# Attention output projection from 16-bit high and low parts; row maxima as bias of one exponential per head on ScalarE

## The chip, the cores and the metric

The kernel runs on one core of a Trainium2 chip. The metric is the device time of one execution in microseconds (us). The engines are named as the profile names them: PE (TensorE), PEld (its weight loads), DVE (VectorE), ACT (ScalarE), POOL (GpSimd) and SP (SyncE, which issues most of the DMAs).

## The reference

A graph network of four layers over 2048 nodes with 512 features, each with layer norm and ReLU ahead of it and a residual sum behind it. The change touches the first layer alone, an attention over 32 graphs of 64 nodes with 8 heads of 64 features. `eb` is a bias per edge, added to the scores at the edge's place.

```
h = jnp.maximum(_layernorm(x, axis=-1), 0.0)
q = (h @ Wq + bq).reshape(32, 64, 8, 64)      # k and v alike
attn = jnp.einsum('bnhd,bmhd->bnmh', q, k) * scale
attn = attn.at[b_idx, loc_src, loc_dst].add(eb)
attn = jax.nn.softmax(attn, axis=2)
out = jnp.einsum('bnmh,bmhd->bnhd', attn, v).reshape(2048, 512)
x = x + out @ Wo + bo
```

Three graph convolutions follow, each a product with a 512 x 512 weight and a sum over edges by dense 2048 x 2048 matrices that the kernel builds itself.

## The kernel before

The program has three stretches. First it reads the edges, builds count, weight and bias matrices and projects q, k and v (to about 424 us of the span). Then comes the attention. Then come the layers, which are long runs of 16-bit matmuls.

The attention works on 16 tiles of 128 nodes (two graphs each). Its order is written out by hand as a pipeline: `attention_periods` runs t from -4 to 16, and in each period every engine does a fixed list of steps for different tiles, with semaphores between them. In period t

- PE turns the probabilities of tile t+1 (`turn`, L1628), projects the output of tile t with Wo (`output`, L1658), mixes the values of tile t+1 (`mix`, L1646) and makes the scores of tile t+4 (`scores`, L1617);
- ACT copies the turned probabilities of tile t+1 from PSUM (`copy_turned`, L1556), takes the exponential of tile t+3 (`exponentials`, L1550), and copies the mixed values of tile t+1 with the bias bv added (`copy_mixed`, L1565), which makes `att_t`, the stationary operand of the output projection;
- DVE makes the probabilities of tile t+2 (sum, reciprocal, product, a copy of one head: L1708 to L1717), adds the edge bias to the scores of tile t+3, reduces their maxima per row and head and subtracts them (L1692, L1697, L1700), and adds the projected output of tile t-1 to x with its layer norm statistics (`add_out`, L1723 to L1728);
- POOL adds the row bo to x (L1541).

An engine takes its list in order: a step that waits holds back all that stands behind it. The probabilities have four buffers (`m.prob[:, t % 4]`), `att_t` has one. The output projection is done in f32: Wo (`keep.wo`) and `att_t` are f32 and each tile takes `KT` = 4 matmuls of 128x128 by 128x512.

In the first periods only some of the lists exist: ACT and DVE begin with tiles 0 and 1, PE's first output stands in period 0. In the last four periods steps of the next stage are woven in: DVE's `weight_peak` (L2607), `weight_line` and `weight_spread`, PE's `peak_row` and `peak_all`, ACT's first `relu` and `weight_hi`. `peak_all` stands ahead of `output(14)` on PE and waits for `weight_line` on DVE. The first product of the layers is L2405.

## Time and profile before

| | us |
|---|---|
| median of 3 runs | 1372.05 (1370.95 to 1372.5) |
| the profiled execution | 1371.25, its span 1369.7 |
| PE busy | 1329.6 (97%) |
| DVE busy | 907.8 (66%) |
| ACT busy | 633.8 (46%) |
| POOL busy | 86.9 (6%) |
| matmuls of the output projection (L1658) | 58.8 busy, 602 ns each, 128 passes |

The profile is of one execution. Times in it count from the start of the span. The output projection's 64 f32 matmuls appear as 128, since each is run in two passes. Matmuls overlap, so the mean duration of one is longer than the distance between two. A number in brackets behind a row is the idle time of the engine ahead of it and what ended it.

### The profile page before, as it was taken

How to read it: one execution, taken by the hardware profiler on the slowest of the kernel's cores; microseconds unless marked ns; L12 is line 12 of the kernel's file. 1: busy time of each engine (PE TensorE's matmuls, PEld its weight loads, DVE VectorE, ACT ScalarE, POOL GpSimd, SP SyncE). 2: the span in 40 equal slices, each digit the busy share in tenths (PEclk: the TensorE clock that was granted, in tenths of full speed). 3: DMA queues.
4: the chain of work that ended last, by engine and by line, in shares of the span. 5: the costliest groups of instructions: out<-in, count | busy, mean ns of one | idle time of the engine just before them, and what ended most of it. 6: DMA issues, size and time to landing. Idle time of an engine off the chain costs nothing.

```text
span 1369.7 us, 26459 instructions
## 1 busy us (share of the span) xinstructions
PE 1329.6 (97%) x11088; PEld 822.8 (60%) x11088; DVE 907.8 (66%) x1370; ACT 633.8 (46%) x1073; POOL 86.9 (6%) x79
## 2 busy tenths in 40 slices
PE   8889999989998999999999999999999999999998
PEld 8788899889997665444444444444444445344443
DVE  7898998999997887788768766432354223522423
ACT  2676666556655447863366434211262224422322
POOL 3120010011001120000000001011100000000000
PEclk9899999999999999999999999999999999999999
DMA  9633444344438651100000002032220323463201
GB/s 333 238 111 123 146 151 135 120 131 138 151 132 284 195 196 71 33 0 31 1 1 1 1 31 85 0 86 62 70 62 0 85 70 102 175 230 103 83 0 62
DMA packets 77813, 137.98 MB, mean 101 GB/s; under 512 B 18261, under 2 KB 30677, under 8 KB 76151
## 3 DMA queue, kind: packets, MB, share of 16 engines
q1 hardware_dynamic: 75022, 125.06, 27.8%
q0 software_dynamic: 1280, 5.77, 1.5%
q10 hardware_dynamic: 1384, 5.38, 1.1%
q8 instruction: 90, 1.47, 0.5%
q14 instruction: 37, 0.30, 0.1%
HBM read 82.85 MB, written 53.33 MB: 99 GB/s over the span
## 4 chain that ended last, share of the span: by engine, by line
PE 83%; DVE 11%; ACT 2%; issue 2%; DMA 1%; POOL 0%; ACTq 0%; DVEq 0%; SPq 0%; POOLq 0%
PE banks L2507 16%; PE banks L2446 14%; PE banks L2405 13%; PE banks L2557 12%; PE banks L1242 6%; PE banks L1658 4%; DVE x_sb L881 3%; PE banks L1179 3%; PE banks L1196 2%; PE banks L1253 2%; PE banks L1153 2%; DVE x_sb L864 1%; PE banks L2342 1%; PE banks L1628 1%; PE banks L1646 1%
## 5 line engine op out<-in xcount | busy, mean ns | idle before, releaser
L2507 PE MATMUL banks<-g,count 128*128 128x512 f16 x1024 | 227.1, 379 | 0.0
L2405 PE MATMUL banks<-w_parts,h_parts 128*128 128x512 f16 x960 | 215.8, 379 | 4.2 <-DVE h_parts L2645 2.4
L2507 PEld LDWEIGHTS banks<-g,count 128*128 128x128 f16 x1024 | 99.9, 98 | 113.2
L2557 PE MATMUL banks<-g,part 128*128 128x512 f16 x768 | 165.9, 379 | 0.0
L2405 PEld LDWEIGHTS banks<-w_parts,h_parts 128*128 128x128 f16 x960 | 90.7, 98 | 119.9 <-issue 9.7
L881 DVE TENSOR_TENSOR x_sb<-eb_parts,x_sb 128x4096 f16<-128x4096 f16 x64 | 145.8, 2278 | 0.0
L1242 PE MATMUL banks<-x_sb 128*128 128x128 f16 x2048 | 126.9, 221 | 11.8 <-DVE x_sb L881 11.8
L1242 PEld LDWEIGHTS banks<-x_sb 128*128 128x128 f16 x2048 | 120.9, 99 | 15.2 <-DVE x_sb L881 14.1
L2557 PEld LDWEIGHTS banks<-g,part 128*128 128x128 f16 x768 | 75.1, 98 | 90.6
L3010 DVE SCALAR_TENSOR_TENSOR part<-count,e_scale,part 128x1024 f16<-128x1024 f32 x29 | 37.2, 1284 | 105.9 <-ACT part L2292 105.9
L2292 ACT ACTIVATE part<-count,e_scale 128x1024 f16<-128x1024 f32 x29 | 33.3, 1148 | 110.9 <-PE banks L2557 110.9
L864 DVE TENSOR_TENSOR x_sb<-iota_src,keys 128x2048 f16<-128x2048 f16 x64 | 77.6, 1212 | 0.0
L2647 DVE TENSOR_TENSOR h_parts<-h_gcn_t,h_parts 128x512 f16<-128x512 f32 x48 | 39.8, 831 | 43.8 <-ACT h_parts L2121 43.7
L1253 PE MATMUL banks<-x_sb 128*128 128x64 f16 x1024 | 65.1, 190 | 0.0
L1254 PE MATMUL banks<-x_sb 128*128 128x32 f16 x1024 | 64.2, 178 | 0.0
L1253 PEld LDWEIGHTS banks<-x_sb 128*128 128x128 f16 x1024 | 60.8, 97 | 0.5
L1658 PE MATMUL banks<-wo_sb,att_t 128*128 128x512 f32 x128 | 58.8, 602 | 0.4 <-ACT att_t L1565 0.4
L1254 PEld LDWEIGHTS banks<-x_sb 128*128 128x128 f16 x1024 | 59.0, 96 | 0.1
L993 ACT COPY bias<-banks 128x128 f32<-128x128 f32 x64 | 24.9, 389 | 70.9 <-PE banks L1242 70.8
L2446 PE MATMUL banks<-count,g 128*128 128x512 f16 x256 | 57.1, 379 | 0.0
L2446 PE MATMUL banks<-mix,g 128*128 128x512 f16 x256 | 56.9, 379 | 0.0
L2446 PE MATMUL banks<-mix,S 128*128 128x512 f16 x256 | 56.8, 379 | 0.0
(351 smaller groups left out, 2136.1 us busy)
## 6 DMA issues: line engine op xcount, KB each, us to landing
weight_dram<-w_new SPq DMA_DIRECT2D x60, 256.0 KB, 2.7
count<-weight_dram SPq DMA_DIRECT2D x29, 512.0 KB, 7.3
qk_dram<-stage SPq DMA_DIRECT2D x64, 128.0 KB, 3.0
tiles<-x_dram SPq DMA_DIRECT2D x32, 256.0 KB, 3.7
x_dram<-tiles SPq DMA_DIRECT2D x32, 256.0 KB, 2.8
count<-in_x SPq DMA_DIRECT2D x4, 1024.0 KB, 13.3
h<-in_x SPq DMA_DIRECT2D x16, 256.0 KB, 4.4
h_dram<-h_t SPq DMA_DIRECT2D x8, 512.0 KB, 2.9
```

Of the source, the lines that this page charges most:

```text
L864: dve.tensor_tensor(m.hot_src[:, z].rearrange("p g (c two) -> p g c two", two=2), keep.iota_src[:].rearrange("p (c two) -> p c two", two=2 ...
L881: dve.tensor_tensor(m.hot_eb[:, z].rearrange("p g (t c) -> p g t c", t=NT), values, tiles, ALU.mult).then_inc(s["hots"], 1)
L1179: mm = pe.matmul(out, m.h_slab[slab % 2][:, zh, k, tile * P:(tile + 1) * P], keep.wq[:, zw, k, c * SCOLS:(c + 1) * SCOLS], start=n == 0, s ...
L1242: mm = pe.matmul(m.bias_ps[:, 0:NT * H], m.hot_src[:, z, g], parts[:, part], start=g == part == 0, stop=g == BATCH - 1 and part == 1)
L1253: pe.matmul(m.cw_ps[:, g, 0:2 * CCOLS], m.hot_src[:, z, g], m.hot_cw[:, z, g, 0:2 * CCOLS], start=True, stop=False)
L1254: mm = pe.matmul(m.cw_ps[:, g, CCOLS:2 * CCOLS], m.hot_src[:, z, g], m.hot_cw[:, z, g, 2 * CCOLS:CW], start=False, stop=True)
L1658: mm = pe.matmul(m.wo_ps[:, t % 2], m.att_t[:, k, :], keep.wo[:, k, :], start=k == 0, stop=k == KT - 1)
L2405: mm = pe.matmul(out, m.h_parts[:, slot, zh, k], m.w_parts[:, zw, k], start=n == 0 and layer != 3, stop=n == len(passes) - 1)
L2446: mm = pe.matmul(m.agg_ps[:, bank + d], left, right(i), start=new and i == 0 and z == 0, stop=i == HT - 1 and z == 1, skip_group_check=not ...
L2507: mm = pe.matmul(m.agg_ps[:, b], m.count[:, i, c, block], m.g[:, i, z], start=i == 0 and z == 0, stop=i == NT - 1 and z == 1)
L2557: mm = pe.matmul(m.banks[:, b], m.part[:, n % 3, z, b * P:(b + 1) * P], m.g[:, q, gz], start=q == 0 and (z, gz) == (0, 0), stop=q == NT - ...
L2647: dve.tensor_tensor(out, source, hi, ALU.subtract).then_inc(s["lo"], 1)
```

## The change

It has three parts.

The output projection runs on 16-bit operands. Wo is scaled by a power of two that comes from the sum of its squares, and split into a high f16 part and a low f16 part, the remainder (`wo_parts`). The mixed values are split in the same way in each period (`att_t`, now [P, 2, KT, P] in f16). A tile takes twelve matmuls: high by high, high by low, low by high. The scale is taken back when the output is added to x.

The bias bv leaves the copy: bv @ Wo is computed once and added to the row bo.

The row maxima are no longer subtracted on DVE. The scores are held negated, their minimum is reduced, and ACT takes exp(-score + minimum) with the minimum as bias by partitions, so one instruction for each of the 8 heads.

```
 def exponentials(t):
-        act.activation(prob, prob, ACT.Exp).then_inc(s["exped"], 1)
+        for hd in range(H):
+            part = prob[:, hd * GN:(hd + 1) * GN]
+            op = act.activation(part, part, ACT.Exp, bias=m.row_max[:, t % 2, hd:hd + 1], scale=-1.0)
+        op.then_inc(s["exped"], 1)
+    def wo_squares():
+        act.wait_ge(s["in_wo"], 16)
+        act.wait_ge(keep.first["chunk"], LAST)
+        act.activation(m.wo_unread[:], keep.wo[:], ACT.Square, accum_out=m.wo_square).then_inc(s["wo_squared"], 1)
+    def wo_high():
+        act.wait_ge(s["wo_scaled"], 1)
+        for k in range(KT):
+            act.activation(m.wo_parts[:, 0, k], keep.wo[:, k], ACT.Copy, scale=m.wo_scale).then_inc(s["wo_high"], 1)
 def copy_mixed(t):
-        for k in range(KT):
-            op = act.activation(m.att_t[:, k].rearrange("p (g n) -> p g n", g=2), m.av_ps[:, :, k * GN:(k + 1) * GN],
-                                ACT.Identity, bias=keep.bv_col[:, k:k + 1])
-        op.then_inc(s["copied_av"], 1)
+        for g in range(2):
+            act.activation(att_part(m, 0, g), av_half(m, g), ACT.Copy, scale=m.att_scale).then_inc(s["copied_av"], 1)
...
 # PE
 def mix(t):
-            pe.wait_ge(s["copied_av"], t)
+            pe.wait_ge(s["av_low"], 2 * t)
 def output(t):
-        pe.wait_ge(s["copied_av"], t + 1)
+        pe.wait_ge(s["copied_av"], 2 * t + 2)
...
+        for n, (za, zw) in enumerate(((0, 0), (0, 1), (1, 0))):
+            if za:
+                pe.wait_ge(s["av_low"], 2 * t + 2)
+            for k in range(KT):
+                mm = pe.matmul(m.wo_ps[:, t % 2], m.att_t[:, za, k, :], m.wo_parts[:, zw, k, :], start=n == k == 0, stop=za == 1 and k == KT - 1)
+    def wo_total():
+        pe.wait_ge(s["wo_squared"], 1)
+        pe.matmul(m.wo_ps[:, 0, 0:1], keep.one.to_broadcast([P, P]), m.wo_square, start=True, stop=True)
+        for k in range(KT):
+            mm = pe.matmul(m.wo_ps[:, 1], keep.bv_col[:, k:k + 1].to_broadcast([P, P]), keep.wo[:, k], start=k == 0, stop=k == KT - 1)
+        mm.then_inc(s["wo_total"], 1)
...
 # DVE
 def scores(t):
+        if t >= 2:
+            dve.wait_ge(s["exped"], t - 1)
...
-        dve.tensor_reduce(m.row_max[:, j], p3, axis=AX.X, op=ALU.max).then_inc(s["dve"], 1)
...
-        dve.tensor_tensor(p3, p3, m.row_max[:, j].unsqueeze(2).to_broadcast([P, H, GN]), ALU.subtract).then_inc(s["lowered"], 1)
+        dve.tensor_reduce(m.row_max[:, j], p3, axis=AX.X, op=ALU.min).then_inc(s["lowered"], 1)
 def add_out(t):
-        dve.tensor_tensor(keep.x[:, t, :], keep.x[:, t, :], m.wo_ps[:, t % 2], ALU.add).then_inc(s["wo_done"], 1)
+        dve.scalar_tensor_tensor(keep.x[:, t, :], m.wo_ps[:, t % 2], m.wo_undo, keep.x[:, t, :], ALU.mult, ALU.add).then_inc(s["wo_done"], 1)
+    def wo_powers():
+        dve.wait_ge(s["wo_total"], 1)
+        dve.wait_ge(s["in_bo"], 16)
+        dve.tensor_tensor(m.bo_row[:], m.bo_row[:], m.wo_ps[:, 1], ALU.add)
+        settle(dve.tensor_copy(m.wo_undo, m.wo_ps[:, 0, 0:1]))
...
+    def wo_low():
+        for k in range(KT):
+            dve.wait_ge(s["wo_high"], k + 1)
+            dve.scalar_tensor_tensor(m.wo_parts[:, 1, k], keep.wo[:, k], m.wo_scale, m.wo_parts[:, 0, k], ALU.mult, ALU.subtract).then_inc(s["wo_low"], 1)
+    def att_low(t):
+        for g in range(2):
+            dve.wait_ge(s["copied_av"], 2 * t + g + 1)
+            dve.scalar_tensor_tensor(att_part(m, 1, g), av_half(m, g), m.att_scale, att_part(m, 0, g), ALU.mult, ALU.subtract).then_inc(s["av_low"], 1)
```

`wo_squares` is called in ACT's period -4, `wo_total` at the end of PE's period -3, `wo_powers` in DVE's period -3, `wo_high` and `wo_low` in period -2, `att_low(t + 1)` in each of DVE's periods behind `add_out(t - 1)`. POOL waits for `wo_scaled`, the end of `wo_powers`, in place of bo_row's DMA.

Where the instructions stand. ACT at the start of the attention, before (prob is the scores, then the exponentials; prob_t the turned probabilities; att_t the mixed values):

```order
L1550 ACTIVATE prob<-prob 128x512 x2
L1556 COPY prob_t<-banks 128x512 x2
L1550 ACTIVATE prob<-prob 128x512
L1565 ACTIVATE att_t<-banks,bv_col 128x128 x4
L1556 COPY prob_t<-banks 128x512 x2
L1550 ACTIVATE prob<-prob 128x512
L1565 ACTIVATE att_t<-banks,bv_col 128x128 x4
```

And now (wo_parts is Wo's high part, w_small holds the scales):

```order
L1575 ACTIVATE wo_unread,w_small<-wo_sb 128x2048
L1568 ACTIVATE prob<-prob,row_max 128x64 x16
L1581 ACTIVATE wo_parts<-wo_sb,w_small 128x512 x4
L1587 COPY prob_t<-banks 128x512 x2
L1568 ACTIVATE prob<-prob,row_max 128x64 x8
L1596 ACTIVATE att_t<-banks,w_small 128x4x64 x2
L1587 COPY prob_t<-banks 128x512 x2
L1568 ACTIVATE prob<-prob,row_max 128x64 x8
L1596 ACTIVATE att_t<-banks,w_small 128x4x64 x2
```

The exponentials of tiles 0 and 1 stand behind the Square of Wo, Wo's high parts ahead of the first turned copy, and each later group of eight exponentials ahead of the two high parts of att_t.

DVE at the start, before, from the scores of tile 1 to the probabilities of tile 1:

```order
L1692 SCALAR_TENSOR_TENSOR prob<-bias,scale,banks 128x4x64 x2
L1697 TENSOR_REDUCE row_max<-prob 128x8
L1700 TENSOR_TENSOR prob<-prob,row_max 128x512
L1708 TENSOR_REDUCE row_sum<-prob 128x8
L1711 RECIPROCAL row_sum<-row_sum 128x8
L1714 TENSOR_TENSOR prob<-prob,row_sum 128x512
L1717 COPY prob<-prob 128x64
L1708 TENSOR_REDUCE row_sum<-prob 128x8
```

And now, from the last three of the nine instructions of `wo_powers` (w_small holds the scales; the first six, with the addition to bo_row, stand right ahead):

```order
L1805 TENSOR_SCALAR w_small<-w_small 128x1
L1806 TENSOR_SCALAR w_small<-w_small 128x1
L1807 TENSOR_SCALAR w_small<-w_small 128x1
L1740 SCALAR_TENSOR_TENSOR prob<-bias,scale,banks 128x4x64 x2
L1744 TENSOR_REDUCE row_max<-prob 128x8
L1752 TENSOR_REDUCE row_sum<-prob 128x8
L1755 RECIPROCAL row_sum<-row_sum 128x8
L1758 TENSOR_TENSOR prob<-prob,row_sum 128x512
L1761 COPY prob<-prob 128x64
L1813 SCALAR_TENSOR_TENSOR wo_parts<-wo_sb,w_small,wo_parts 128x512 x4
L1752 TENSOR_REDUCE row_sum<-prob 128x8
L1755 RECIPROCAL row_sum<-row_sum 128x8
```

The nine instructions stand between the reduction of tile 0's scores and the scores of tile 1. Behind the probabilities of tile 0 there follow the four low parts of Wo (L1813), and only then the probabilities of tile 1.

DVE in one period of the steady part, before:

```order
L1692 SCALAR_TENSOR_TENSOR prob<-bias,scale,banks 128x4x64 x2
L1697 TENSOR_REDUCE row_max<-prob 128x8
L1700 TENSOR_TENSOR prob<-prob,row_max 128x512
L1723 TENSOR_TENSOR x_sb<-x_sb,banks 128x512
L1725 BN_STATS stats_101<-x_sb 128x6
L1728 BN_AGGR stats_101<-stats_101 128x2
L1708 TENSOR_REDUCE row_sum<-prob 128x8
```

And now:

```order
L1740 SCALAR_TENSOR_TENSOR prob<-bias,scale,banks 128x4x64 x2
L1744 TENSOR_REDUCE row_max<-prob 128x8
L1767 SCALAR_TENSOR_TENSOR x_sb<-banks,w_small,x_sb 128x512
L1769 BN_STATS stats_101<-x_sb 128x6
L1772 BN_AGGR stats_101<-stats_101 128x2
L1819 SCALAR_TENSOR_TENSOR att_t<-banks,w_small,att_t 128x4x64 x2
L1752 TENSOR_REDUCE row_sum<-prob 128x8
```

The subtraction is gone, and the two low parts of att_t stand between the statistics and the next tile's probabilities.

## Rows read from the trace of the kernel before

**Rows 1.** The page, busy time of each engine in the whole span:
```profile
PE 1329.6 (97%) x11088; PEld 822.8 (60%) x11088; DVE 907.8 (66%) x1370; ACT 633.8 (46%) x1073; POOL 86.9 (6%) x79
```

**Rows 2.** Busy time by stretches: stretch, its length, then each engine, granted clock, DMA:
```profile
72.00:78.00 6.00, 3.67 (x72) 3.52 (x73) 6.00 (x10) 5.15 (x11) 0.00 (x0) 1.00 0.47 160
431.05:437.63 6.58, 5.85 (x80) 5.18 (x81) 5.64 (x11) 2.79 (x8) 2.95 (x2) 0.60 1.03 352
441.38:509.02 67.64, 67.64 (x882) 42.46 (x880) 59.49 (x124) 31.35 (x77) 14.08 (x11) 1.00 0.64 209
```

**Rows 3.** The chain of waits in order of time: start, length, what:
```profile
466.58 0.73 PE banks L1646 x24
467.49 0.76 PE banks L1617 x28
...
469.27 3.44 PE banks L1658 x8
```

**Rows 4.** The timeline of one period: start, length, engine, line, operation:
```profile
459.83 0.65 DVE L1708 TENSOR_REDUCE row_sum<-prob 128x8 f32<-128x512 f32 x1
...
461.42 1.15 ACT L1565 ACTIVATE att_t<-banks,bv_col 128x128 f32<-128x128 f32 x4 [2.38 <-PE banks L1646]
...
462.17 0.87 DVE L1692 SCALAR_TENSOR_TENSOR prob<-bias,scale,banks 128x256 f32<-128x256 f32 x2 [0.50 <-PE banks L1617]
...
463.08 0.69 DVE L1697 TENSOR_REDUCE row_max<-prob 128x8 f32<-128x512 f32 x1
...
463.80 0.69 DVE L1700 TENSOR_TENSOR prob<-prob,row_max 128x512 f32<-128x512 f32 x1
...
464.41 0.68 DVE L1723 TENSOR_TENSOR x_sb<-x_sb,banks 128x512 f32<-128x512 f32 x1
464.53 0.63 ACT L1550 ACTIVATE prob<-prob 128x512 f32<-128x512 f32 x1 [0.70 <-DVE prob L1700]
...
465.95 0.65 DVE L1708 TENSOR_REDUCE row_sum<-prob 128x8 f32<-128x512 f32 x1
```

**Rows 5.** The timeline, TensorE in the layers behind the attention:
```profile
541.38 2.76 PE L2405 MATMUL banks<-w_parts,h_parts 128*128 128x512 f16 x12 [0.25 <-DVE h_parts L2647]
543.99 1.04 PE L2342 MATMUL banks<-ident,h_gcn 128*128 128x128 f32 x8
```

**Rows 6.** Groups by form on ScalarE: count, busy us, mean ns, idle before:
```profile
L1565 ACT ACTIVATE att_t<-banks,bv_col 128x128 f32<-128x128 f32 x64 | 18.3, 368 | 34.2 <-PE banks L1646 34.2
...
L1057 ACT ACTIVATE stage<-banks,bq_col,w_small 128x256 f32<-128x256 f32 x28 | 15.6, 566 | 11.7 <-PE banks L1196 11.7
L1063 ACT ACTIVATE stage<-banks,w_small 128x256 f32<-128x256 f32 x32 | 15.1, 476 | 11.1 <-PE banks L1179 11.1
...
L1550 ACT ACTIVATE prob<-prob 128x512 f32<-128x512 f32 x16 | 10.1, 631 | 15.5 <-DVE prob L1700 15.5
...
L1026 ACT ACTIVATE w_slab<-w_slab 128x2048 f32<-128x2048 f32 x1 | 1.9, 1911 | 0.0
```

**Rows 7.** Groups by form on VectorE:
```profile
L2934 DVE SCALAR_TENSOR_TENSOR tiles<-banks,odis1u,tiles 128x512 f32<-128x512 f32 x16 | 12.0, 751 | 54.2 <-PE banks L2507 37.0 <-POOL tiles L2057 17.2
```

**Rows 8.** The timeline at the start of the attention:
```profile
424.48 2.42 ACT L988 ACTIVATE x_sb<-banks,scale 128x512 f32<-128x512 f32 x4 [1.17 <-PE banks L1153]
...
430.91 0.68 DVE L1708 TENSOR_REDUCE row_sum<-prob 128x8 f32<-128x512 f32 x1
...
434.07 2.95 POOL L1541 TENSOR_TENSOR x_sb<-x_sb,bo_row 128x512 f32<-128x512 f32 x2 [109.32 <-DMA bo_row<-in_L_gnn_bo]
...
436.58 0.69 DVE L1708 TENSOR_REDUCE row_sum<-prob 128x8 f32<-128x512 f32 x1 [0.69 <-ACT prob L1550]
```

**Rows 9.** The timeline at the end of the attention:
```profile
514.91 2.25 DVE L2607 TENSOR_REDUCE peak<-w_raw 128x1 f32<-128x2048 f32 x1
...
528.37 1.10 ACT L1565 ACTIVATE att_t<-banks,bv_col 128x128 f32<-128x128 f32 x4
...
534.92 2.75 PE L2405 MATMUL banks<-w_parts,h_parts 128*128 128x512 f16 x12
```

More of the change, by code:

```diff
@@ L1444, in attention_memory @@
     m.bo_row = place("bo_row", [P, D], F32, AT_REST + 20992)
-    m.att_t = place("att_t", [P, KT, P], F32, AT_REST + 23552)
+    m.att_t = place("att_t", [P, 2, KT, P], F16, AT_REST + 23552)
+    m.wo_parts = place("wo_parts", [P, 2, KT, D], F16, AT_SLAB)
+    m.wo_unread = place("wo_unread", [P, KT, D], F32, AT_SLAB)
+    m.wo_square, m.att_scale, m.wo_undo = (keep.w_squares[:, i:i + 1] for i in range(1, 4))
+    m.wo_scale, m.wo_down = (keep.w_squares[:, i:i + 1] for i in range(4, 6))
     m.moments = m.stats[:, 6 * NT:8 * NT].rearrange("p (t two) -> p t two", two=2)
@@ L1448, in attention_memory @@
     m.s_ps = keep.banks[:, 6:8].rearrange("p o (j n) -> p o j n", j=2)
-ATTENTION_SEMS = ("in_wo in_bo plus wo score score_read lowered exped prob turned copied_prob weighed copied_av wo_done var std normed dve "
+ATTENTION_SEMS = ("in_wo in_bo plus wo score score_read lowered exped prob turned copied_prob weighed copied_av av_low wo_squared wo_total wo_scaled wo_high wo_low wo_done var std normed dve "
                   "in_qk0 in_qk1 in_v0 in_v1 out_deg in_deg deg deg_root dis out_dis in_dis " + " ".join(f"in_x{i}" for i in range(SLABS)) + " " + " ".join(f"out_x{i}" for i in range(4)))
 SHORT = NT - 3
+ATT_SHIFT = 2.0 ** -4
 FIRST = -4
@@ L1525, in attention_sp @@
     sp.wait_ge(s["out_dis"], 16)
+    sp.wait_ge(s["wo"], NT)
     sp.dma_start(layers.dis_row[:], io["dis_dram"][0:1].to_broadcast([P, N])).then_inc(s["in_dis"], 16)
@@ L1528, in attention_sp, with av_half, att_part @@
         sp.wait_ge(s[f"out_x{i}"], 16 * NT // 4)
+def av_half(m, g):
+    return m.av_ps[:, g, 0:KT * GN].rearrange("p (k n) -> p k n", k=KT)
+def att_part(m, z, g):
+    return m.att_t[:, z].rearrange("p k (g n) -> p g k n", g=2)[:, g]
 def attention_pool(nc, io, keep, m, s):
     pool = nc.gpsimd
-    pool.wait_ge(s["in_bo"], 16)
+    pool.wait_ge(s["wo_scaled"], 1)
     for t in range(NT):
@@ L1574, in attention_act @@
             copy_turned(t + 1, 1)
+        if t == FIRST:
+            wo_squares()
         if is_tile(t + 3):
             exponentials(t + 3)
+        if t == -2:
+            wo_high()
         if t == NT - 2:
@@ L1676, in attention_pe @@
             scores(t + 4)
+        if t == -3:
+            wo_total()
 def attention_dve(nc, io, keep, layers, m, s, tools):
@@ L1690, in scores @@
             dve.wait_ge(s["turned"], 2 * (t - 4) + 2)
+        if t >= 2:
+            dve.wait_ge(s["exped"], t - 1)
         for odd in range(2):
[L1692 to L1694 removed]
+            op = dve.scalar_tensor_tensor(p3.rearrange("p (h o) m -> p o h m", o=2)[:, odd], bias.rearrange("p (h o) t m -> p o h t m", o=2)[:, odd, :, t],
+                                          keep.scale[:, 2:3], m.s_ps[:, odd, j].rearrange("p (h m) -> p h m", m=GN), ALU.mult, ALU.subtract)
         op.then_inc(s["score_read"], 1)
         dve.wait_ge(s["score_read"], t + 1)
[L1697 to L1700 removed]
+        dve.tensor_reduce(m.row_max[:, j], p3, axis=AX.X, op=ALU.min).then_inc(s["lowered"], 1)
     def probabilities(t):
@@ L1743, in norm, with settle @@
         dve.scalar_tensor_tensor(keep.shift[:, tiles], m.moments[:, tiles, 0], -1.0, keep.rstd[:, tiles], ALU.mult, ALU.mult).then_inc(s["normed"], 1)
+    def settle(op):
+        nonlocal n_dve
+        op.then_inc(s["dve"], 1)
+        n_dve += 1
+        dve.wait_ge(s["dve"], n_dve)
+    def wo_powers():
+        up, down = m.wo_scale.bitcast(I32), m.wo_down.bitcast(I32)
+        dve.wait_ge(s["wo_total"], 1)
+        dve.wait_ge(s["in_bo"], 16)
+        dve.tensor_tensor(m.bo_row[:], m.bo_row[:], m.wo_ps[:, 1], ALU.add)
+        settle(dve.tensor_copy(m.wo_undo, m.wo_ps[:, 0, 0:1]))
+        settle(dve.tensor_scalar(down, m.wo_undo.bitcast(I32), 24, None, ALU.logical_shift_right))
+        settle(dve.tensor_scalar(up, down, -1, 204, ALU.mult, ALU.add))
+        settle(dve.tensor_scalar(down, down, 50, None, ALU.add))
+        dve.tensor_scalar(up, up, 23, None, ALU.logical_shift_left)
+        settle(dve.tensor_scalar(down, down, 23, None, ALU.logical_shift_left))
+        dve.tensor_scalar(m.att_scale, keep.w_powers[:, 2:3], ATT_SHIFT, None, ALU.mult)
+        dve.tensor_scalar(m.wo_undo, m.wo_down, keep.w_powers[:, 5:6], 1.0 / ATT_SHIFT, ALU.mult, ALU.mult).then_inc(s["wo_scaled"], 1)
+    def wo_low():
[6 more added lines that the diff above has]
+            dve.scalar_tensor_tensor(att_part(m, 1, g), av_half(m, g), m.att_scale, att_part(m, 0, g), ALU.mult, ALU.subtract).then_inc(s["av_low"], 1)
     for t in attention_periods():
@@ L1746, in attention_dve @@
             tools.start()
+            settle(dve.tensor_scalar(keep.scale[:, 2:3], keep.scale[:, 2:3], -1.0, None, ALU.mult))
         if t == NT - 4:
@@ L1769, in attention_dve @@
             tools.split_lo(0, 1)
+        if t == -3:
+            wo_powers()
+        if t == -2:
+            wo_low()
         if is_tile(t - 1):
             op = add_out(t - 1)
+        if is_tile(t + 1):
+            att_low(t + 1)
         if t == NT - 4:
@@ L2464, in paired_sums @@
                 pe.wait_ge(keep.attention_sems["wo_done"], NT)
[L2465 removed]
+                pe.wait_ge(keep.attention_sems["av_low"], 2 * NT)
                 pe.wait_ge(s["looped"], HT * (h + 1))
```

11 lines of the change are left out of this document (2 added, 9 removed).

## The prediction

> **What bounds the kernel now.** I read the page first: TensorE is busy for 97% of the span and VectorE for 66% [rows 1]. The change touches one stage, the attention, so I then took the busy times by stretches. From 441.38 to 509.02 us TensorE has no idle time at all, VectorE is busy 59.5 of 67.6 us, ScalarE 31.4, and the granted clock is 1.00, the 2.4 GHz level [rows 2]. The reader is to see that TensorE alone bounds this stretch. The chain of waits in order of time splits one tile: the mix from 466.58, the scores from 467.49, then the turn, the output projection from 469.27 to 472.71, and the next mix at once. A tile takes 6.12 us, and 3.44 of that are the four f32 matmuls with Wo (two passes of 0.43 us each) [rows 3].
>
> Then I read VectorE and ScalarE over one period, since they become the question once TensorE needs less [rows 4]. VectorE starts a tile at 459.83 and the next at 465.95. In between: probabilities 1.84 us (459.83 to 461.67), an idle 0.50 us waiting for the scores, the two score instructions and the maximum (start to start 0.91 and 0.72), the subtraction (0.61 until the next start), and the addition of the output with its statistics (464.41 to 465.95, 1.54). That is 5.62 us of work in 6.12: only half a microsecond is free. ScalarE has much room, but it works in a fixed order, and its exponential starts only when VectorE has lowered the scores (0.70 us of idle time ends there).
>
> **What the change does to one period.** TensorE: four f32 matmuls of 3.44 us become twelve of 16 bits. Twelve of just that form take 2.61 us in the layers (they start at 541.38, and the turn behind them at 543.99) [rows 5]. TensorE's need falls from 6.12 to 5.3 us. If it stayed the bound, each period would gain 0.83 us.
>
> VectorE: the subtraction goes (0.72 after the reduction it depends on). The addition becomes a scalar-tensor-tensor, 0.75 against 0.68 us by the form of L2934 [rows 7], so 1.61 for this part. Two low parts are added, 128x256 each, read from PSUM with a scalar: the two score instructions are the same size and take 0.87 together, a start each 0.39. The sum is 1.79 + 0.91 + 0.61 + 1.61 + 0.78 = 5.70 us (1.79 is the probabilities with the tail of the last copy overlapped). So VectorE's need alone is above TensorE's.
>
> ScalarE: one exponential of 128x512 at 0.63 us becomes eight of 128x64 with a bias by partitions. No row has that form, so I work it out. The exponential of 512 columns without a scalar operand takes 631 ns; an instruction of 256 takes 476 with one and 566 with two, so a scalar adds 90; from 128 to 256 columns with one (368 and 476) a column costs 0.84 ns [rows 6]. 631 + 90 - 448 x 0.84 = 345 ns each. The four of L1565 are 368 ns each and 1.15 us together, so each starts 0.10 us before its predecessor ends [rows 4, 6]. Eight then hold the engine for 8 x 0.25 = 2.00 us. The lower bound is the spacing in L1565, 0.26, less 64 columns, 0.21 each, 1.7 in all; the upper is no overlap, 2.8. I take 2.00, since like instructions overlap in this very stage.
> The Trainium skill's page "ScalarE: Activation LUTs", section "Rules for kernel authors", says to budget about 0.3 us for each ACTIVATE with a bias operand besides its elements; taken so, an estimate for eight is 2.8 us, which would make each period 0.8 us longer than what I forecast. The 1.15 us for four in this trace speak against it; the rule names no overlap.
> The four biased copies (1.15) become two copies of 128x256 with a scale, by L1063 476 ns each [rows 6], the second 0.38 behind the first.
>
> Now the order decides. VectorE's period t is: probabilities(t+2), scores(t+3), addition(t-1), low parts(t+1). ScalarE's is: copies of the turned tile t+1, exponentials(t+3), high parts(t+1). The new low parts wait for the high parts, these stand behind the eight exponentials on ScalarE, and the exponentials wait for the minimum that VectorE has just reduced. That closes a loop within one period. Before, the copy behind the exponential only fed TensorE, which was busy anyway. The loop: probabilities 1.79, scores 0.91, minimum until seen 0.71, eight exponentials 2.00, first high part 0.48, second 0.38, seen 0.04, second low part's start-to-start 0.39. Sum 6.70 us. The addition (1.61) lies beside the exponentials and costs nothing; VectorE idles 1.0 us a period and TensorE 1.4. What queues behind the waiting low part on VectorE is the next tile's probabilities, so the whole pipeline takes the delay. A period grows from 6.12 to 6.70.
> Bounds by the exponential: 6.4 and 7.5.
>
> **The start of the stage.** Work is added here on the path. ScalarE ends the last copies at 426.90 [rows 8], then the Square of Wo: 1.91 us for 2048 columns [rows 6] plus about 0.2 for its accumulator, until 429.0. TensorE adds one small and four f32 matmuls, 3.5 us, until 432.5. They lie in a stretch where it idles now, and this is hidden by something later: VectorE's new chain waits for bo_row, and that DMA landed at 434.07, where GpSimd was released [rows 8]. So the powers run from 434.05: one 128x512 addition (0.61) and eight tiny instructions that wait for each other (about 0.17), 1.95 in all, until 436.0. Only then come scores(1) (0.91) and the minimum (0.61), until 437.5, and probabilities(0), until 439.3. Behind exponentials(1) (437.6 to 439.65) ScalarE makes the high parts of Wo, four at 0.61 (476 ns and 256 more columns, less the overlap); VectorE's low parts follow from 440.4, four at 0.67 (0.75 less an overlap of 0.08, as between the two score instructions), until 443.06. There probabilities(1) starts; in the trace of before it starts at 430.91 [rows 8]. That is 12.15 us late. One round of 6.70 (probabilities, scores, the exponentials, the first high and low parts) brings probabilities(2) to 449.8, against 436.58 [rows 8]: 13.2 late. The first output projection then runs at the lower clock level, as TensorE has been waiting: before, 431.05 to 437.63 was granted 0.60 after its waits [rows 2]. Twelve matmuls at half speed take 5.1 instead of 2.6, the mix behind them delays the first high parts: 0.5 more.
> Bounds: if bo_row lands with the rest and the powers start at 432.5, 1.5 less; if the tiny instructions see each wait late, 1 more.
>
> **Steady part and end.** Twelve periods (t = 0 to 11) at 6.70 from 449.8, with the 0.5, bring VectorE's period 12 to 530.7 and the output of tile 12 to 530.3. Before, that output started at 512.11 (469.27 and seven tiles of 6.12). So TensorE is 18.2 us late there.
> Before, VectorE began a tile's period 3.3 us ahead of its output (459.83 and 469.27 less 6.12), and this hid weight_peak (2.25 us, 514.91 [rows 9]). That lead is gone: low parts(13) at 537.7, weight_peak until 539.9, probabilities(15) until 541.7, addition(12) until 543.3, low parts(14) until 544.1, variance and the weight's line until 545.5. TensorE's peak_all stands ahead of output(14), so it and mix(15) end near 549.5; high parts(15) end at 550.4 instead of 529.5 [rows 9]. ScalarE's work from there to the first product keeps its length: the product at 534.92 [rows 9] comes at about 555.8. The end costs 2.7 more.
> Sum: 18.2 + 2.7 = 20.9 us. Behind the first product the work is the same and TensorE-bound. The profiled execution took 1371.25 us for a span of 1369.7, 0.8 under the median of 1372.05. 1371.25 + 20.9 = 1392.2; I say 1392.5. Its own range: the exponentials give -4 to +10 over 13 periods, the start -1.5 to +1: 1386 to 1402.
>
> **Rivals.**
> TensorE or VectorE stays the bound (the loop is not closed, the exponentials overlap more). With VectorE as bound, 5.70 a period: 13 us less than forecast, so about 1379. For: 5.70 is the work that must be done at least. Against: the four of L1565 show 0.26 each, and the order puts the low parts behind the exponentials. Chance 5%.
> Faster: one mechanism, the start is absorbed. If the new work at the start lay beside what VectorE waits for now and the loop ran at TensorE's 5.3, the 13 periods would give back 10.8 and the outputs 13 to 15 another 2.5. The point from which it decides: with that period, a start that costs under 13.3 us. If it cost 8, the time is 1371.25 + 8 - 13.3 = 1366. Against: bo_row at 434.07 and four low parts ahead of probabilities(1). Chance 3%, and 3% for landing within 0.2%.
> The clock falls in the loop: TensorE would idle 1.4 of 6.7 us. At the 1.2 GHz level its 5.3 us become at most 10.6, 3.9 more than 6.70; in all 13 periods 51 us, 1443, in a third of them about 1409. Against: from 72 to 78 us TensorE was busy 3.67 of 6 us and was granted 1.00 [rows 2]. The Trainium skill, "TensorE: Matmul & The Clock Gate", section "A second HAM failure mode: psum-queue depth-cycling", says that short idle times between groups of matmuls can make the clock go to and fro; by that rule this case is the likely one, by the row it is not. Chance 5%.
> The change doesn't do what it says: the twelve matmuls or the eight exponentials are as described in the order, so I give this nothing apart.
>
> **Chances.** Forecast mechanism 84%, VectorE's bound 5%, clock 5%, within 0.2% 3%, faster 3%. About 0.2% is what a measurement of this kernel can tell from no change. The first three are all slower: 0.94. The range 1383 to 1403 leaves out the rivals and a little of the forecast's own tails.
>
> **What would show it.** Right: output matmuls 0.22 us apart, 12 a tile; eight exponentials in about 2.1 us with ScalarE's wait on the minimum ahead of them; idle time of VectorE ahead of the low parts, about 0.4 to 0.9 us a tile, released by ScalarE; TensorE idle ahead of the output projection; a tile each 6.7 us; clock 1.00 in the steady part; VectorE waiting near 428 to 434 us for bo_row. Wrong: a period of 6.1 or less, exponentials 0.15 or 0.35 us apart, probabilities(1) before 440 us, or the loss lying behind the first product of the layers.

## The result and the profile after

The changed kernel took 1393.73 us (median of 4 runs, 1392.69 to 1394.4), the kernel before beside it 1371.5 (1368.68 to 1372.5). The recorded ratio is 1.0173, 95% interval 1.0153 to 1.0192 (the two medians alone give 1.0162, inside the interval). The profiled execution took 1393.9 us, its span 1392.6. The forecast was 1392.5, range 1383 to 1403.

The page, busy time of each engine:

```profile
PE 1327.0 (95%) x11162; PEld 821.2 (59%) x11162; DVE 913.5 (66%) x1400; ACT 651.5 (47%) x1159; POOL 85.6 (6%) x79
```

Against [rows 1], TensorE is busy 2.6 us less in a span 22.9 longer. Its busy time did not grow; its waiting did. The stretches of the changed kernel (stretch, length, each engine, granted clock, DMA):

```profile
430.00:436.00 6.00, 3.95 (x8) 1.38 (x6) 1.33 (x7) 0.23 (x1) 0.00 (x0) 0.85 0.94 305
442.00:448.00 6.00, 3.31 (x65) 3.01 (x66) 4.83 (x10) 2.36 (x8) 1.26 (x1) 0.50 0.01 3
466.00:524.00 58.00, 47.51 (x749) 31.16 (x746) 48.61 (x106) 33.17 (x108) 11.06 (x9) 1.00 0.61 198
542.00:548.00 6.00, 4.09 (x12) 1.72 (x13) 4.73 (x21) 3.73 (x10) 0.00 (x0) 0.72 0.21 78
```

In the steady part TensorE is busy 47.5 of 58 us, where it had no idle time before [rows 2]. One period, timeline:

```profile
492.56 0.69 DVE L1744 TENSOR_REDUCE row_max<-prob 128x8 f32<-128x512 f32 x1
...
493.16 0.74 DVE L1767 SCALAR_TENSOR_TENSOR x_sb<-banks,w_small,x_sb 128x512 f32<-128x512 f32 x1
493.28 2.02 ACT L1568 ACTIVATE prob<-prob,row_max 128x64 f32<-128x64 f32 x8 [2.93 <-DVE row_max L1744]
...
495.21 0.81 ACT L1596 ACTIVATE att_t<-banks,w_small 128x256 f16<-128x256 f32 x2
495.69 0.88 DVE L1819 SCALAR_TENSOR_TENSOR att_t<-banks,w_small,att_t 128x256 f16<-128x256 f32 x2 [0.84 <-ACT att_t L1596]
...
496.07 2.76 PE L1694 MATMUL banks<-wo_parts,att_t 128*128 128x512 f16 x12 [1.17 <-ACT att_t L1596]
496.49 0.68 DVE L1752 TENSOR_REDUCE row_sum<-prob 128x8 f32<-128x512 f32 x1
...
498.27 0.87 DVE L1740 SCALAR_TENSOR_TENSOR prob<-bias,scale,banks 128x256 f32<-128x256 f32 x2
499.18 0.69 DVE L1744 TENSOR_REDUCE row_max<-prob 128x8 f32<-128x512 f32 x1
```

Read it by who releases whom: VectorE's minimum releases the exponentials (ScalarE idle 2.93 us), they hold back the high parts of att_t, these release VectorE's low parts (idle 0.84) and TensorE's output (idle 1.17), and only behind the low parts stands the next sum. From minimum to minimum it is 6.62 us.

VectorE at the start, by the timeline:

```profile
434.53 0.69 DVE L1799 TENSOR_TENSOR bo_row<-bo_row,banks 128x512 f32<-128x512 f32 x1 [9.47 <-DMA bo_row<-in_L_gnn_bo]
...
437.82 0.68 DVE L1752 TENSOR_REDUCE row_sum<-prob 128x8 f32<-128x512 f32 x1
...
440.61 3.07 DVE L1813 SCALAR_TENSOR_TENSOR wo_parts<-wo_sb,w_small,wo_parts 128x512 f16<-128x512 f32 x4 [0.92 <-ACT wo_parts L1581]
443.60 0.67 DVE L1752 TENSOR_REDUCE row_sum<-prob 128x8 f32<-128x512 f32 x1
...
450.20 0.67 DVE L1752 TENSOR_REDUCE row_sum<-prob 128x8 f32<-128x512 f32 x1
```

And TensorE at the end, the outputs of tiles 12 to 14:

```profile
529.13 2.76 PE L1694 MATMUL banks<-wo_parts,att_t 128*128 128x512 f16 x12 [1.16 <-ACT att_t L1596]
...
535.99 2.76 PE L1694 MATMUL banks<-wo_parts,att_t 128*128 128x512 f16 x12 [2.16 <-ACT att_t L1596]
...
543.91 0.38 PE L2438 MATMUL banks<-line,ones 1*128 1x8 f32 x2 [2.30 <-DVE line L2672]
544.23 4.45 PE L1694 MATMUL banks<-wo_parts,att_t 128*128 128x512 f16 x12
```

The first product of the layers starts at 555.92, against 534.92 [rows 9]: 21.0 us late, where the two spans differ by 22.9. The missing 1.9 us lie in the layers behind it: this execution took 836.7 us from the first product to its end, the one before 834.8, for the same matmuls. Of these, 1.7 lie at one place. There TensorE waited 2.04 us and was granted 0.50 behind the wait; at the same place the kernel before waited 1.66 us and kept 1.00.

```profile
854.42 0.60 PE L2488 MATMUL banks<-w_parts,h_parts 128*128 128x512 f16 x2 [2.04 <-DVE h_parts L2728]
...
856.00:858.00 2.00, 2.00 (x6) 0.63 (x5) 1.57 (x4) 2.00 (x4) 0.00 (x0) 0.50 0.14 55
```

### The profile page after: what moved, and what is told of

Its sections match the earlier page's. It is cut to its first block, busy times and chain, and to the rows that moved or that the text cites. A ratio compares the mean times of both kernels' runs of the same rounds, so it can differ in the third digit from the quotient of the medians.

```text
span 1392.6 us, 26729 instructions
## 1 busy us (share of the span) xinstructions
PE 1327.0 (95%) x11162; PEld 821.2 (59%) x11162; DVE 913.5 (66%) x1400; ACT 651.5 (47%) x1159; POOL 85.6 (6%) x79
## 4 chain that ended last, share of the span: by engine, by line
PE 75%; DVE 16%; ACT 4%; issue 2%; DMA 1%; SPq 0%; ACTq 0%; POOL 0%; DVEq 0%; POOLq 0%
PE banks L2590 16%; PE banks L2529 14%; PE banks L2488 13%; PE banks L2640 12%; PE banks L1242 6%; DVE x_sb L881 3%; PE banks L1179 3%; PE banks L1196 2%; PE banks L1253 2%; ACT prob L1568 2%; PE banks L1153 2%; DVE x_sb L864 1%; PE banks L2425 1%; PE banks L290 1%; DVE prob L1740 1%
## 5 line engine op out<-in xcount | busy, mean ns | idle before, releaser
L1694 PE MATMUL banks<-wo_parts,att_t 128*128 128x512 f16 x192 | 47.1, 398 | 15.0 <-ACT att_t L1596 15.0
```

Of the source, the lines that this page charges most:

```text
L1694: mm = pe.matmul(m.wo_ps[:, t % 2], m.att_t[:, za, k, :], m.wo_parts[:, zw, k, :], start=n == k == 0, stop=za == 1 and k == KT - 1)
```

## The experiments

The kernel before ran in each of the four sets: 1369.04 (rows 2 to 5 of the table), 1371.1 (rows 6 to 9), 1370.3 (rows 10 to 12) and 1368.92 us (the last row). The third and the fourth set ran on other chips than the first two. Ratios are to the kernel before of the same set, so across sets compare ratios. "Period" is the distance between two tiles in the profile's steady part.

| run | median us | ratio, 95% interval | period us |
|---|---|---|---|
| the change | 1393.73 | 1.0173 (1.0153 to 1.0192) | 6.62 |
| subtraction kept, one exponential | 1389.06 | 1.0146 (1.0123 to 1.0168) | 6.39 |
| before, with the eight exponentials alone | 1369.87 | 1.0001 (0.9989 to 1.0013) | 6.12 |
| low parts a step later | 1379.32 | 1.0068 (1.0048 to 1.0088) | 5.66 |
| four exponentials | 1382.86 | 1.0096 (1.0077 to 1.0116) | 5.88 |
| start reordered | 1383.57 | 1.0100 (1.0085 to 1.0115) | 6.62 |
| start and low parts | 1372.46 | 1.0010 (1.0000 to 1.0019) | 5.66 |
| these, scores ahead | 1389.45 | 1.0135 (1.0120 to 1.0151) | 6.97 |
| these, sums on ScalarE | 1379.36 | 1.0062 (1.0044 to 1.0080) | 6.25 |
| scores, low parts, probabilities | 1375.8 | 1.0035 (1.0019 to 1.0052) | 5.69 |
| the same, sums on ScalarE | 1366.46 | 0.9967 (0.9952 to 0.9982) | 5.27 |
| the same, start freed | 1361.89 | 0.9942 (0.9926 to 0.9958) | 5.27 |
| before, sums on ScalarE | 1371.51 | 1.0018 (1.0006 to 1.0030) | 6.12 |

### Which part closes the loop

The 16-bit projection with the old softmax:

```
-        for hd in range(H): ... ACT.Exp, bias=m.row_max[...], scale=-1.0
+        act.activation(prob, prob, ACT.Exp, scale=-1.0)          # and on DVE, behind the minimum:
+        dve.tensor_tensor(p3, p3, m.row_max[:, j]...broadcast, ALU.subtract)
```

> The changed kernel with one part undone: DVE subtracts the row minima again and ACT takes one exponential of 128x512 per tile; the 16-bit output projection stays. My theory (a tile's period is the longer of two sums, the loop DVE minimum - eight exponentials - high parts - low parts, now 6.62 us, and DVE's own work): the loop falls to 1.79 + 0.91 + 0.72 + 0.71 + 0.53 + 0.49 + 0.79 = 5.9 us, but DVE's work rises to 1.79 + 0.91 + 0.72 + 0.61 + 1.61 + 0.78 = 6.4 us and becomes the bound. Period 6.4, no idle time of DVE, total about 1390 us. Rival (the eight exponentials are the whole loss of the steady part): period 6.1 or less, total 1387 us or less.

1389.06 us and 6.39: the loop lost its exponentials, but the subtraction came back, and VectorE works through a period without a wait:

```profile
492.81 0.84 DVE L1819 SCALAR_TENSOR_TENSOR att_t<-banks,w_small,att_t 128x256 f16<-128x256 f32 x2
493.56 0.68 DVE L1752 TENSOR_REDUCE row_sum<-prob 128x8 f32<-128x512 f32 x1
...
499.95 0.68 DVE L1752 TENSOR_REDUCE row_sum<-prob 128x8 f32<-128x512 f32 x1
```

So the projection and its start lose 20 us also without the eight exponentials, but by another bound. The difference to the change is therefore not the price of the exponentials in the changed kernel; the run with four of them, below, shows that price.

The other part alone, on the kernel before:

```
-        act.activation(prob, prob, ACT.Exp)
+        (eight exponentials as in the change; minimum, no subtraction)
```

> The kernel before with the other part alone: row minima as bias of eight exponentials per tile, no subtraction on DVE, output projection in f32 as before. My theory: nothing on DVE waits for the copies of the mixed values, so the loop isn't closed; PE stays the bound with 6.12 us a tile, ACT's added 1.4 us lie beside it, total 1371 to 1373 us, within 0.2% of before. Rival (1.4 us more of exponentials per tile cost by themselves): 0.5 to 1.4 us a tile, 1379 to 1393 us.

1369.87 and 6.12, no difference. The exponentials cost only where something that TensorE needs stands behind them. The period of that run (timeline):

```profile
484.19 1.14 ACT L1568 ACTIVATE att_t<-banks,bv_col 128x128 f32<-128x128 f32 x4 [1.72 <-PE banks L1649]
...
486.58 2.02 ACT L1552 ACTIVATE prob<-prob,row_max 128x64 f32<-128x64 f32 x8
488.62 0.69 DVE L1710 TENSOR_REDUCE row_sum<-prob 128x8 f32<-128x512 f32 x1 [0.54 <-ACT prob L1552]
```

VectorE even waits 0.54 us for them, and it costs nothing, since TensorE is busy in all of the 38 us from 466 to 504.

The low parts of tile t taken in period t, behind the scores, not in period t-1 behind the exponentials:

```
-        if is_tile(t + 1):
-            att_low(t + 1)      # behind add_out(t - 1)
+        if is_tile(t):
+            att_low(t)          # behind scores(t + 3)
```

> The changed kernel with one move: DVE makes the low parts of tile t (not t+1) in period t, behind the scores of tile t+3. They then wait for high parts that ACT finished a period earlier. My theory: the loop over ACT is gone, DVE's work of 5.7 us a tile is the bound, 0.9 us less over 12 to 13 periods, total about 1382 us, the start of the stage as in the changed kernel. Rival (PE's restarts after idle time, or ACT's load, hold the period): 6.1 us or more, 1387 us or more.

1379.32 and 5.66, which is VectorE's own work (5.70 by the forecast, and no row of VectorE from 480 to 495 us has a wait); about 1382 us had been expected. Nothing else differs from the change, so the loop is shown, and its share of the loss is 14 us. By the traces 12.6 of them lie between the probabilities of tile 2 and of tile 15, the rest ahead of and behind that stretch.

```profile
483.81 0.65 DVE L1752 TENSOR_REDUCE row_sum<-prob 128x8 f32<-128x512 f32 x1
484.34 0.84 ACT L1596 ACTIVATE att_t<-banks,w_small 128x256 f16<-128x256 f32 x2 [0.78 <-PE banks L1679]
485.57 0.87 DVE L1740 SCALAR_TENSOR_TENSOR prob<-bias,scale,banks 128x256 f32<-128x256 f32 x2
...
487.08 0.86 DVE L1819 SCALAR_TENSOR_TENSOR att_t<-banks,w_small,att_t 128x256 f16<-128x256 f32 x2
487.20 2.02 ACT L1568 ACTIVATE prob<-prob,row_max 128x64 f32<-128x64 f32 x8 [0.46 <-DVE row_max L1744]
...
489.47 0.65 DVE L1752 TENSOR_REDUCE row_sum<-prob 128x8 f32<-128x512 f32 x1
```

The low parts have no wait in brackets any more: the high parts they need were made 2 us earlier.

Four exponentials of 128x128, with one minimum for two heads:

```
-        for hd in range(H): part = prob[:, hd * GN:(hd + 1) * GN]
+        for pair in range(H // 2): part = prob[:, pair * 2 * GN:(pair + 1) * 2 * GN]
```

> The changed kernel with the minimum reduced over pairs of heads (128 columns) and four exponentials of 128x128 per tile instead of eight of 128x64; order as in the changed kernel. My theory: four hold ACT for 4 x 0.30 = 1.2 us instead of 1.93, all of it in the loop, so the period falls from 6.62 to 5.9 us, DVE's idle time ahead of the low parts from 0.84 to 0.1 us, total about 1384 us. Rival (the period is set by the waits between the engines and not by the number of exponentials): 6.4 us or more, 1391 us or more.

1382.86 and 5.88. The four took 1.28 us, the eight 2.02, and the period fell by the same 0.74: what the exponentials take, the loop takes.

```profile
483.71 1.28 ACT L1568 ACTIVATE prob<-prob,row_max 128x128 f32<-128x128 f32 x4 [2.92 <-DVE row_max L1745]
```

### The start

The sum of squares signalled ahead of bv @ Wo; the powers behind scores(1), without bo_row; bo_row's sum and Wo's low parts in period -1; GpSimd released by that sum; output(0) waits for the low parts only ahead of its second group.

```
+        if t == -2:
+            wo_powers()         # no wait for in_bo in it
+        if t == -1:
+            bo_sum(); wo_low()
```

> The changed kernel with only its start reordered: PE gives the total of the squares its own signal ahead of the bv @ Wo matmuls, DVE makes the powers behind the scores of tile 1 and no longer waits there for bo_row, the addition to bo_row and the low parts of Wo stand in period -1 beside the exponentials of tile 2, and output(0) waits for the low parts only at its second group of four. Steady part and end as in the changed kernel. My theory (11 us of the 13 that the start costs are DVE waiting for bv @ Wo and bo_row's DMA and then for Wo's high parts): the probabilities of tile 2 start near 439.5 us instead of 450.2, total 10 to 11 us under the changed kernel, 1382 us. Rival (the start's loss is hidden by TensorE's later work or is a loss of the clock after idle time): under 5 us, 1388 us or more.

1383.57, 10.2 us less than the change. Probabilities(2) began at 438.46 instead of 450.20, and the first product at 544.12 instead of 555.92. But 3.1 us of both lie ahead of the stage, since the minimum of tile 0 was reduced at 421.29 in this execution and at 424.37 in the one of the changed kernel. Counted from that minimum, the new start gains 8.7 us. Both moves together, the two edits above unchanged:

> Both moves together: the reordered start and the low parts of tile t in period t. My theory: the two losses are separate and add up, 10.9 us less than the kernel with the low parts moved alone (1379.3), total about 1368.5 us, no slower than before. Rival (they share a cause, so the second removal gives less): 1374 us or more.

1372.46, at most 0.2% above the kernel before, where 1368.5 was expected. The moves gave back 21.3 of 22.2 us. The trace is of the slowest of twelve executions (1374.94). From the minimum of tile 0 to the first product it is 19.4 us shorter than the changed kernel, where the two moves alone save 14.4 and 8.7. Its start (timeline, and one row by stretches):

```profile
430.41 5.23 PE L1704 MATMUL banks<-wo_sb,bv_col 128*128 128x512 f32 x8
435.58 0.98 PE L1650 MATMUL banks<-qk_second 64*64 64x64 f32 x32
...
438.71 4.76 DVE L1819 SCALAR_TENSOR_TENSOR wo_parts<-wo_sb,w_small,wo_parts 128x512 f16<-128x512 f32 x4
438.88 3.38 POOL L1557 TENSOR_TENSOR x_sb<-x_sb,bo_row 128x512 f32<-128x512 f32 x2 [112.94 <-DVE bo_row L1813]
...
447.60 1.89 PE L1696 MATMUL banks<-wo_parts,att_t 128*128 128x512 f16 x4 [3.03 <-DVE att_t L1825]
...
447.00:453.00 6.00, 5.40 (x72) 3.90 (x72) 2.90 (x8) 2.65 (x10) 1.26 (x1) 0.52 0.14 25
```

Of the 3.7 us that are missing from the sum, 2.3 lie in one period: the last four matmuls of output(0) waited 3.03 us for the low parts of att_t, TensorE was granted about half its clock behind that wait, and probabilities(4) came 7.94 us behind probabilities(3) instead of 5.66. The other 1.4 lie ahead of probabilities(2). Two more costs of the start are seen in these rows. Scores(2) waited for bv @ Wo on TensorE, and the four low parts of Wo ran beside GpSimd's sums and took 4.76 us. The second is not part of what was missing, since the run with the start alone has the same 4.76 us.

### A second loop, and its order undone

Two runs were to relieve VectorE further: scores(t+3) ahead of probabilities(t+2), alone and with the row sums taken by the exponentials.

```
+        if is_tile(t + 3):
+            scores(t + 3)       # ahead of probabilities(t + 2) in every period
# second run, also:
+            ... ACT.Exp, bias=..., scale=-1.0, accum_out=m.row_sum[:, t % 2, hd:hd + 1])
-        dve.tensor_reduce(m.row_sum[:, j], p3, axis=AX.X, op=ALU.add)
```

> As the kernel with both moves, with DVE making the scores of tile t+3 ahead of the probabilities of tile t+2 and nothing else, so that the exponentials of a tile have a whole period of DVE. My theory: with the low parts moved, DVE's own work is already the bound and no wait of the exponentials is left, so nothing changes: 5.66 us a tile, 1368.5 us, the same as with both moves within 1 us. Rival (a wait on the exponentials is still in the period): 0.2 us a tile or more less, 1366 us or less.

> As the kernel with both moves, and in addition DVE makes the scores of tile t+3 ahead of the probabilities of tile t+2, and the eight exponentials sum their heads themselves (accum_out), so DVE's reduction of the row sums (0.7 us) goes. My theory: DVE's work falls from 5.66 to about 5.0 us a tile, TensorE with 5.3 us is the bound again, 0.3 to 0.4 us a tile less, total about 1364 us, faster than both kernels. Rival (the sums make the exponentials 2.7 us and more, and ACT or a loop over it is the bound): 5.7 us or more a tile, 1368 us or more.

Both missed: 1389.45 with 6.97 us, where 5.66 was expected, and 1379.36 with 6.25, where TensorE's need of 5.3 was expected. The timeline of the first:

```profile
479.57 0.87 DVE L1742 SCALAR_TENSOR_TENSOR prob<-bias,scale,banks 128x256 f32<-128x256 f32 x2 [1.20 <-PE banks L1650]
...
481.08 0.68 DVE L1754 TENSOR_REDUCE row_sum<-prob 128x8 f32<-128x512 f32 x1
...
482.86 0.87 DVE L1825 SCALAR_TENSOR_TENSOR att_t<-banks,w_small,att_t 128x256 f16<-128x256 f32 x2
...
483.79 1.04 PE L1696 MATMUL banks<-wo_parts,att_t 128*128 128x512 f16 x4 [1.52 <-DVE att_t L1825]
484.75 0.80 PE L1679 MATMUL banks<-prob_t,v 64*64 64x64 f32 x26
485.56 0.92 PE L1650 MATMUL banks<-qk_first 64*64 64x64 f32 x29
...
486.53 0.87 DVE L1742 SCALAR_TENSOR_TENSOR prob<-bias,scale,banks 128x256 f32<-128x256 f32 x2 [1.20 <-PE banks L1650]
```

The last four matmuls of the output wait for the low parts, behind them on TensorE stand the mix (L1679) and the scores (L1650), and VectorE waits for these scores. The probabilities lie ahead of the low parts and so in this loop. With the sums on ScalarE it is shorter by 0.72, which is the 0.71 us of the sum within the rounding. To test this, the low parts go ahead of the probabilities:

```
+        if is_tile(t):
+            att_low(t)          # now between scores(t + 3) and probabilities(t + 2)
```

> The kernel that put VectorE's scores(t+3) ahead of its probabilities(t+2), with one call moved: the low parts of tile t now stand between the two. Theory: that kernel's 6.97 us came from a loop through TensorE (scores 0.9, minimum 0.6, probabilities 1.8, low parts 0.9, the last four output matmuls, mix 0.9, scores 0.9); with the probabilities out of this loop it measures 5.2 us or less, and VectorE's own 5.66 us of work sets the period again: 5.7 us, and about 1372 us, 17 less than with the probabilities in the loop. Rival: early scores cost time for another reason (the exponentials, or TensorE's order); the period stays at 7.0 us and the time at 1389.

The period is 5.69, and VectorE waits for nothing in it:

```profile
478.14 0.86 DVE L1825 SCALAR_TENSOR_TENSOR att_t<-banks,w_small,att_t 128x256 f16<-128x256 f32 x2
...
479.06 1.04 PE L1696 MATMUL banks<-wo_parts,att_t 128*128 128x512 f16 x4 [0.24 <-DVE att_t L1825]
```

The loop is gone, and the profiled run took the expected 1372.5. The median was 1375.8: its twelve times fall in two groups, 1370.4 to 1372.5 and 1374.8 to 1378.7, the lower with the higher clock over the run (0.989 to 0.993 against 0.984 to 0.989). With the sums on ScalarE:

> The same, with the row sums taken by the exponentials themselves (eight times 0.33 us of exponential plus 0.10 us for reading the sum, 2.78 us in place of 2.02) and VectorE's sum of 0.71 us gone. VectorE's work is 4.95 us a tile, TensorE needs 5.3, the loop through TensorE 5.2 to 5.4. Theory: period 5.4 us, 13 periods of 0.25 us less than with the sums on VectorE: about 1369 us. Rival: ScalarE's longer exponentials delay the high parts and through them the output product; period 5.7 or more, 1372 or later.

1366.46 and 5.27, with TensorE busy in all of 38 us:

```profile
466.00:504.00 38.00, 38.00 (x618) 26.15 (x615) 35.16 (x84) 33.32 (x142) 9.16 (x8) 1.00 0.72 245
```

This is the first kernel here that is faster than before, by 0.33%. Its period is what the prediction had put down as TensorE's need, 5.3 us from [rows 5]. Then the two conflicts of the start were taken away:

```
+        if t == -2:
+            bo_product()        # bv @ Wo, behind scores(2)
-    pool.wait_ge(s["bo_sum"], 1)
+    pool.wait_ge(s["wo_low"], KT)
```

> The same as the run with sums on ScalarE, with two moves at the start: the product of the value bias and Wo, 5.2 us on TensorE, is issued behind scores(2) instead of ahead of them, and GpSimd's first sums wait until the low parts of Wo are there, so that they don't run beside them (4.76 us for four low parts beside GpSimd, where four measured 3.07 in the changed kernel and one alone 0.67). Theory: the start was held by these two, and 2 to 4 us come off: about 1366 us, below both kernels. Rival: the start is held by the chain from Wo's squares and powers to its high parts, which neither move touches: no difference, 1369.

1361.89, 0.58% below the kernel before. The low parts ran alone:

```profile
437.63 2.73 DVE L1820 SCALAR_TENSOR_TENSOR wo_parts<-wo_sb,w_small,wo_parts 128x512 f16<-128x512 f32 x4
...
440.45 2.51 POOL L1557 TENSOR_TENSOR x_sb<-x_sb,bo_row 128x512 f32<-128x512 f32 x2 [115.64 <-DVE wo_parts L1820]
```

But in the traces little of the stage's time is saved: on VectorE it is 21.6 us from the minimum of tile 0 to the scores of tile 4 (424.88 to 446.44), and 21.9 in the run without these moves (423.64 to 445.57). The product took 6.02 us, since TensorE was granted 0.50 when it began, and VectorE waited 1.70 for it; without the moves the product took 3.68. The rest of the 4.6 us between the medians goes with the clock over the run: without the moves seven of twelve executions took 1366 to 1368 us at 0.988 or 0.989 and five 1360 to 1366 at 0.992 and above, this version 1362 to 1363 at 0.990 to 0.992. The two intervals overlap, and what the moves are worth stays open.

Last, whether the sums on ScalarE would have done without the 16-bit projection:

> The kernel before with its 32-bit projection kept, eight exponentials with the minimum as bias, and the row sums taken by these exponentials. VectorE's work falls by the subtraction and the sum (0.7 us each) to 4.1 us a tile. Theory: TensorE bounds the 32-bit kernel (it is busy in 43.0 of the 43.0 us of its steady stretch), so nothing is gained: period 6.12 us, 1370 us, and the gain of the fastest version needs the 16-bit projection as well. Rival: VectorE's or ScalarE's chain sets 6.12 us too, and the period falls (VectorE's relief) to 5.6 or rises (exponentials 0.8 us longer) to 6.5.

1371.51, period 6.12: no gain, perhaps 0.2% lost. Its steady part has VectorE busy 25.5 us, where the kernel before has 33.5 in the same stretch, and TensorE has no room:

```profile
466.00:504.00 38.00, 38.00 (x507) 24.37 (x502) 25.49 (x56) 30.86 (x137) 8.82 (x7) 1.00 0.71 220
```

## Why the prediction was right, step by step

The mechanism was right: the loop, its terms, the wait for bo_row and the lost lead at the end are all in the trace. That the forecast was only 1.2 us under the measured time is in part luck, since errors of 0.4 to 1.7 us cancelled on the way to the first product.

| from the start of the span, later than before | forecast | measured |
|---|---|---|
| probabilities(2) | 13.2 | 13.6 |
| output of tile 12 | 18.2 | 17.0 |
| first product of the layers | 20.9 | 21.0 |
| end of the span | 20.9 | 22.9 |

**The period.** Forecast 6.70, measured 6.62. Added from the rows above: probabilities 1.78 (496.49 to 498.27), scores 0.91, minimum until seen 0.72 (492.56 to 493.28), exponentials until the first high part 1.93 (forecast 2.00), first high part until the low parts 0.48, low parts until the next sum 0.80 (0.81). Only the exponentials differ by more than 0.01: they took 334 ns each, against 345 worked out, and the first high part overlaps the last of them too. The rule of the Trainium skill ("ScalarE: Activation LUTs", "Rules for kernel authors") of 0.3 us for each ACTIVATE gives, as an estimate, 2.8 us for eight; the measured 2.02 contradicts it as a sum. The Trainium skill has, on the same page under "What ACT_TABLE_LOAD costs", what was overlooked: 280 ns plus 0.833 ns a column with a bias by pointer, and back-to-back instructions overlap by 93 ns. As an estimate from these, one takes 333 ns and eight take 2.0 us; this trace agrees with both.

**That the loop bounds, not VectorE.** Shown by moving the low parts alone (5.66). The rival with VectorE as bound, 1379 us, is what that run measured: the bound was right, the order kept the kernel from reaching it.

**The start.** Forecast bo_row at 434.05, probabilities(1) at 443.06, probabilities(2) at 449.8. Measured 434.53, 443.60 and 450.20. VectorE's 9.47 us wait was ended by the DMA, as forecast. The sum had 3.5 us for the small and the four f32 matmuls and their end at 432.5. The four alone took 5.11 us and ended at 433.95, since the stretch from 429.5 to 431 was granted 0.50 and the next 1.5 us 0.75; the DMA covered that. The low parts of Wo took 3.07 us, not 2.66. TensorE was granted 0.50 from 442 to 452, and the first output took 3.94 us. The 0.5 us that had been put down for this did not come: probabilities(3) began at 456.80, 6.60 behind probabilities(2).

**The end.** Output(12) came at 529.13, forecast 530.3: 1.0 less by twelve shorter periods and 0.5 less by the delay that did not come, against 0.4 more from the start. From there to the first product the prediction had 2.7 us more than before; it was 4.0 (21.0 less the 17.0 by which output(12) was late against 512.11). Here a term was missing. TensorE waited 2.30 us for the weight's line, the stretch from 542 to 548 was granted 0.72, and output(14) took 4.45 us instead of 2.76. Against these 1.7 us the weight's line was ready at 543.85 instead of 545.5, mostly by the shorter periods. The two cancel, and the first product came at 555.92 against 555.8 forecast. That this number is so near is luck.

**Behind the first product.** The prediction put nothing here. The work is the same, but the traces differ by 1.9 us, most of it where the granted clock fell to 0.50 in the layers (854.42 and 856.00 above). Of the fourteen profiled executions ten took 834.3 to 835.1 us for this stretch, the kernel before and both fastest versions among them. The changed kernel and the runs with one exponential, with the low parts a step later and with scores, low parts, probabilities took 836.1 to 836.8. The run with four exponentials has the changed kernel's order and took 834.8. So this cost does not come in each execution; what decides it is not shown.

**The clock rival.** TensorE idled about 1.2 of each 6.6 us, and the steady part was granted 1.00 throughout, the 2.4 GHz level. The Trainium skill ("TensorE: Matmul & The Clock Gate", "A second HAM failure mode: psum-queue depth-cycling") has the clock go to and fro over short idle times between groups of matmuls; in the steady part this trace does not agree. In the order with the second loop the idle time was 1.52 us and the grant was 1.00 too. In the changed kernel the clock fell behind waits of 2.00, 3.38, 2.30 and 2.04 us. So the rival was wrong as a mechanism of the steady part, but a lower clock did cost time at the end and in the layers, where the prediction had no term for it.

**The rival faster than before** named the start as the point that decides. The start alone did not decide: with it and with VectorE's 5.66 a period the time came out level. Faster came only with the sums off VectorE as well, when the period was the 5.3 us that this rival asks for.

## What to carry to other kernels

Before an engine's work is made shorter, look for the loop that closes when a step moves to an engine whose list has another long step ahead of it: add its terms from one result to the same result of the next tile, and compare with each engine's own work. The cure of the loop was the place of one call, taking the dependent step a period later. The next move in the order closed another loop, so the sum has to be made again for each order. An operation that is free beside a bound engine (eight exponentials, 0 us) can cost all that it takes once something needed stands behind it (2.02 us against 1.28 made 0.74 us a period).
